# The device loop over the middle tiles of a fused Mamba and mixture-of-experts layer, written out as one straight list of steps on every engine

## The reference

```python
x = x + mamba(layernorm(x));  x = x + moe(layernorm(x))

def mamba(x):
    u, res = split(x @ W_in);  u = silu(u)
    delta = softplus(u @ W_delta + b_delta);  Bm = u @ W_B;  Cm = u @ W_C
    h = exp(delta * A) * h + delta * Bm * u          # a scan over the 256 tokens, for 16 states
    y = sum over states of h * Cm, plus u * D_param
    return (y * silu(res)) @ W_out

def moe(x):
    gate = x @ Wg.T + routing_bias
    weights = softmax over the 4 largest of 8 gates
    return swiglu(x, Ws1, Ws2, Ws3) + sum_e weights[e] * swiglu(x, W1[e], W2[e], W3[e])
    # swiglu(u, w1, w2, w3) = (silu(u @ w1.T) * (u @ w2.T)) @ w3.T
```

## Time and profile before

| what | value |
|---|---|
| three runs | 1539.65, 1535.20, 1539.01 us; median 1539.01 us |
| the profiled execution, whole | 1535.95 us |
| its span, first to last instruction | 1534.1 us |
| what lies around the span | 1.85 us |
| granted TensorE clock, mean | 0.988 of full speed |
| PE busy | 1473.8 us, 96% of the span |
| DVE busy | 1413.0 us, 92% |
| ACT busy | 1230.3 us, 80% |
| POOL busy | 850.2 us, 55% |

### The profile page before, as it was taken

How to read it: one execution, slowest core, us unless ns; L and a number is a source line. 1 busy time by engine, 2 the same in 40 slices (tenths; PEclk the granted TensorE clock), 3 DMA queues, 4 the chain that set the end, 5 groups by cost and what they waited for, 6 DMA issues and landing times. The chain is left out here.

```text
span 1534.1 us, 31186 instructions
## 1 busy us (share of the span) xinstructions
PE 1473.8 (96%) x9510; PEld 1245.7 (81%) x9510; DVE 1413.0 (92%) x2834; ACT 1230.3 (80%) x1841; POOL 850.2 (55%) x508
## 2 busy tenths in 40 slices
PE   4879999999999999999999999999999999999998
PEld 3677887888788887888879788887978888898887
DVE  5869999999999999999999999999999999999843
ACT  5978888888789798888979888897988889787331
POOL 5965564665456376555647556564755657375100
PEclk7999999999999999999999999999999999999999
DMA  5320212112111211211121131112202120201000
GB/s 183 95 99 22 74 34 81 43 57 77 35 57 43 90 41 37 95 35 56 42 90 41 36 96 35 56 42 70 87 10 87 46 63 29 98 15 57 1 8 8
DMA packets 50482, 87.02 MB, mean 57 GB/s; under 512 B 4663, under 2 KB 32820, under 8 KB 50356
## 3 DMA queue, kind: packets, MB, share of 16 engines
q1 hardware_dynamic: 49556, 82.52, 16.6%
q10 hardware_dynamic: 800, 3.14, 0.6%
HBM read 80.93 MB, written 4.72 MB: 56 GB/s over the span
## 5 line engine op out<-in xcount | busy, mean ns | idle before, releaser
L641 POOL TENSOR_TENSOR hb<-soft,bbc 128x1024 f32<-128x1024 f32 x256 | 628.2, 2479 | 21.4 <-DMA bbc<-b_rows 18.3
L1131 PEld LDWEIGHTS eo_bank<-w_sb,gated 128*128 128x128 f32 x3840 | 470.5, 192 | 30.6 <-issue 17.5
L1131 PE MATMUL eo_bank<-w_sb,gated 128*128 128x128 f32 x3840 | 488.2, 276 | 2.7 <-DVE o L937 1.9
L861 DVE SCALAR_TENSOR_TENSOR acc<-turn,c_sb,acc 128x256 f32<-128x256 f32 x900 | 375.9, 474 | 13.3 <-issue 10.6
L696 ACT ACT_TABLE_LOAD x299 | 383.6, 1283 | 5.4
L849 DVE TENSOR_TENSOR_SCAN hb<-decay_bank,hb 128x512 f32<-128x512 f32 x256 | 310.7, 1214 | 24.3 <-POOL hb L641 14.1
L1064 PE MATMUL turn<-ident,hb 128*128 128x128 f32 x2048 | 291.6, 275 | 36.1 <-DVE hb L849 16.9
L794 ACT ACTIVATE s<-h 128x512 f32<-128x512 f32 x384 | 221.8, 598 | 126.8 <-PE h L1115 121.0
L849 DVE TENSOR_TENSOR_SCAN hb<-decay,hb 128x512 f32<-128x512 f32 x256 | 318.3, 1274 | 2.0 <-ACT decay L776 1.8
L1064 PEld LDWEIGHTS turn<-ident,hb 128*128 128x128 f32 x2048 | 241.9, 142 | 82.8 <-issue 22.5
L928 DVE TENSOR_TENSOR gated<-h,s 128x512 f32<-128x512 f32 x384 | 253.5, 678 | 28.0 <-PE h L1115 17.6
(11 more groups left out here) (105 smaller groups left out, 1511.2 us busy)
## 6 DMA issues: line engine op xcount, KB each, us to landing
bbc<-b_rows SPq DMA_DIRECT2D x128, 512.0 KB, 5.1
x_in<-x_dram SPq DMA_DIRECT2D x16, 256.0 KB, 3.0
x_cur<-x_dram SPq DMA_DIRECT2D x16, 256.0 KB, 6.3
out_dram<-o SPq DMA_DIRECT2D x15, 256.0 KB, 2.5
gated<-w_all_dram ACTq DMA_DIRECT2D x1, 1534.5 KB, 8.6
hb<-w_all_dram ACTq DMA_DIRECT2D x1, 1534.5 KB, 12.4
w_sb<-w_all_dram SPq DMA_DIRECT2D x5, 192.0 KB
b_rows<-cbT SPq DMA_DIRECT2D x16, 32.0 KB, 1.6
```

Of the source, the lines that this page charges most:

```text
L641: pool.tensor_tensor(hb[:, arg % HB_RING, :, :], du[:, h, :].unsqueeze(1).broadcast_to((P, GN, TOK)), bbc[:, r, :].rearrange("p (n t) -> p ...
L861: dve.scalar_tensor_tensor(acc[:, blk, :], turn_bank[pair][:, i * DI:(i + 1) * DI], c_sb[:, blk, n:n + 1], acc[:, blk, :], ALU.mult, ALU.add)\
L1131: mm = pe.matmul(eo_bank[:, blk * P:(blk + 1) * P], gated[:, k % GATED_RING, blk * P:(blk + 1) * P], w3_sb[:, pair, :], start=(n == 0), st ...
```

## The change

`bodies` now builds one Python list for each engine: the head, then the body nine times with the numbers of its tiles filled in for j = 6 to 14, then the tail. `program` is called once with that list. The tables are the same, so each engine executes the same steps in the same order. What falls away is the device loop itself, all register instructions that computed wait values and addresses in the body, and the special cases at the seams of head, body and tail (which activation table ACT holds there, and which step last used the shared PSUM bank `side` on PE).

```diff
         def bodies(eng, engine, program):
 
             head, body, tail = ORDER[engine]
-            program([((tile, 0), step, arg) for tile, step, arg in head], None)
-            with eng.Fori(*LOOP) as j:
-                program([((j, SHIFT[part]), step, arg) for part, step, arg in body], body)
-            program([((tile, 0), step, arg) for tile, step, arg in tail], body)
+            program([((tile, 0), step, arg) for tile, step, arg in head]
+                    + [((j + SHIFT[part], 0), step, arg) for j in range(*LOOP) for part, step, arg in body]
+                    + [((tile, 0), step, arg) for tile, step, arg in tail])
...
-            def program(entries, before):
-                table = table_after(before, None) if before else EXP_TABLE
-                head = before is None
+            def program(entries):
+                table = EXP_TABLE
                 for turn, step, arg in entries:
...
-                wanted = table_after(ORDER["act"][1], None)
-                if head and table != wanted:
-                    act.preload_act_table_set(wanted)
-
...
-            def program(entries, before):
-                if before is None:
-                    last = None
-                elif isinstance(entries[0][0][0], int):
-                    last = last_side(before, lambda part: (LOOP[1] - 1, SHIFT[part]))
-                else:
-                    side_free(last_side(ORDER["pe"][0], lambda tile: (tile, 0)))
-                    last = last_side(before, lambda part: (entries[0][0][0], SHIFT[part] - 1))
+            def program(entries):
+                last = None
                 for turn, step, arg in entries:
```

More of the change, by code:

```diff
@@ L975, in side_free @@
                     wait_before(pe, reader, turn, per, GATE_STEPS if step == "gate" else arg + 1)
-            def last_side(entries, turn_of):
-                uses = [(turn_of(at), step, arg) for at, step, arg in entries if step in SIDE]
-                return uses[-1]
             def stay_busy(times):
```

## The result

The changed kernel takes 1522.61 us (median of six runs, 1519.87 to 1526.93). Six runs of the kernel before, the three shown above and three beside the changed one, have a median of 1537.57 us (1535.20 to 1540.35). The ratio is 0.9905, with a 95% interval of 0.9887 to 0.9924: about 1% faster. The prediction had the direction right and the size too small.

The account below looks back on a forecast made before the run. PE and DVE, both nearly full in the eight looped passes, were taken as the bound. Only DVE's jumps counted: 8 x 1.29 = 10.3 us off 1539.01 gives 1528.7 us, range about 1524 to 1534 us.

Parts of the forecast that it names:

- The jump back on DVE, eight times, removed: At DVE's loop jump in the middle: removing the code fetch saves 1.29 us a pass, 10.3 us in all.
- The register steps ... Counted at nothing: In the loop body, 140 a pass on DVE and 83 on PE: hidden behind queued work, so removal gains nothing.
- What is late next. PE ... the gain cannot go beyond the 1.29 us: In each middle pass: without the stall PE's own 88.66 us bounds, so the gain stops at 1.29 us.
- Rival 4: In the passes: fewer sequencer steps let DVE and PE start earlier; 88.4 us a pass, gain 12.4 us; chance 0.08.
- Head and tail ... stays: Outside the loop: time unchanged, including PE's 3.03 us wait for ACT's sres before the first pass.
- Straight code must be fetched ... at nothing: In the written-out passes: PE fetches about 5 blocks each, 40 more in all, at no cost.
- Rival 3: In the written-out passes: PE's code blocks arrive late, about 1.3 us each; with two a pass 1549.5 us; chance 0.04.
- The jumps of PE, ACT, POOL and SP: At the other engines' loop jumps: removing them counted at nothing.
- Rival 2: At DVE's stall on sum: it comes with the place, not the jump, and stays; 1538 us; chance 0.05.

Follow-up runs that it names:

- e1: The kernel before, loops kept, without PE's one wait between head and loop body; 1532.13 us, ratio 0.9971.
- e4: The kernel before without PE's wait at the loop's entry, with a prefetch hint on DVE's loop jump; 1528.26 us, ratio 0.9941.
- e8: The changed kernel, but PE loops with a body of three passes and so jumps back twice; 1527.46 us, ratio 0.9919.
- e5: The changed kernel with PE's wait for ACT's sres put back where the head ends; 1527.75 us, ratio 0.9923.
- e2: The kernel before with only DVE's list written out straight; other engines' loops and PE's entry wait stay; 1526.18 us, ratio 0.9919.
- e9: The kernel before without PE's entry wait, DVE's loop cut right behind three queued scans, seven jumps; 1534.26 us, ratio 0.9980.
- e12: The kernel of e9 with DVE's loop head placed at the start of a code block; 1523.30 us, ratio 0.9917.
- e7: The changed kernel, but DVE loops with a body of three passes and so jumps back twice; 1524.58 us, ratio 0.9900.

## Why the prediction was right or wrong

**"The jump back on DVE, eight times, removed": right, and priced somewhat high.** Measured alone (from e1 to e4) it is 1.15 us a pass, between PE's visible wait of 1.10 us and the 1.29 us taken. The 1.29 us was the difference between a later pass and the first; with the wait of PE gone too (e1) it is 89.891 - 88.63 = 1.26 us. The Trainium skill, page "Advanced Engine Details and Errata", section Control Flow Timing, has some 108 ns for a compare-and-branch, which by itself would be 0.9 us in all. The runs disagree with that as the price of a jump whose target is not at hand: 1.15 us each here, 3.9 us each on PE in e8.

**"The register steps ... Counted at nothing": wrong, and the step that made the passes too long.** They cost 0.23 to 0.27 us a pass on DVE, about 2 us in all. The 1.467 us that a pass lost are 1.15 for the fetch, 0.23 for DVE's register steps, 0.03 for the other engines (no more than noise), and 0.05 by which the profiles of before and e1 differ. The "proof" was a mistake of method. I took the first pass as the changed kernel in small and PE's lack of idle time in it as a sign that the steps were covered. But the first pass has the register steps too, so comparing it with a later one cannot show them. And "never idle" is not "as fast as it can be": its 88.66 us became 88.36 without a listed wait of PE having been there to remove. What went were the delays of under 0.1 us by which DVE let PE go late.

**"What is late next. PE ... the gain cannot go beyond the 1.29 us": wrong for the same reason.** PE's 88.66 us were not PE's own. Its matmuls alone need at most the 88.48 us of the changed kernel. Rival 4, which let DVE and PE start earlier for want of sequencer steps and had 88.43 us a pass, had the mechanism and the pass (to 0.05 us), and with its 12.4 us it was closer than the forecast; it had been given 0.08.

**"Head and tail ... stays": wrong, and the step that put the result outside the range.** I read `ACT sres` in the bracket of the earlier trace rows as a dependence of the data. It was a wait emitted at the seam, and the diff shows its removal in PE's program. What the profile names as the releaser says whose event ended the wait, not that the wait is needed. e1 and e5 measure it: 3.2 and 3.0 us in the profiles. With these 3.2 us still there the median would be about 1525.8 us, inside the range.

**"Straight code must be fetched ... at nothing": right.** 38 blocks on q8 in the eight passes, and PE has no listed wait. Rival 3 (late blocks, slower) did not occur. The Trainium skill, page "Runtime: NRT & Kernel Launch", section Instruction fetch mechanics, says that fetching the next block of straight code is mostly hidden, and the changed profile agrees: 38 packets and no wait of PE.

**"The jumps of PE, ACT, POOL and SP": right**, at most 0.03 us a pass with their register steps (e2). For PE that holds only while its body is kept; e8 shows the other side.

**Rival 2, the stall comes with the place:** false. Straight code has none at the same step, and when the jump was moved (e9) the stall moved with it.

Put together: 10.3 forecast, plus 1.4 (passes), plus 3.2 (seam), plus 0.3 (first pass) is 15.2 us; the start's +1.2 us and the rest's -0.3 make it 14.4 in the spans. Those are 4.1 us more than forecast. Between the forecast of 1528.7 us and the median of 1522.61 us lie 6.1 us: 1.4 us more come from the three added runs of the kernel before, which lowered its median, and 0.6 us from the difference between a profiled execution and a median.

## What to carry to other kernels

To price a jump, look at when the engine's sequencer does its next step, and set against it how much work is queued on the engine there; only the difference is lost. Where a loop has to stay, putting the jump right behind long instructions, and the loop's head at the start of a block of code, is worth a try: in this kernel e12 got a looped body to within 0.27 us a pass of straight code. On two engines that are both nearly full, an empty list of waits does not show that neither delays the other; the starts of the same instruction in two traces do. And read every removed line of a diff that emits a wait, also at seams: a wait that the profile puts down to another engine's work may be an instruction that nothing needs.

## What the runs showed that I had not expected

- A wait of some 3 us of TensorE is sometimes followed by several microseconds at half the clock, and sometimes not. After 3.04 us of idle time e2 fell to 0.59 and 0.50 and lost 2.5 us more, and after 2.43 us e8 fell to 0.59 and lost 1.4 us; the kernel before, after 3.03 us, and e5, after 2.8 us, stayed at 1.00. What decides it stays open.
- The stop behind a jump was 3.4 to 3.6 us on DVE in the kernel before, 2.8 to 2.9 us in e7, 3.1 to 3.4 us in e9, 2.8 to 2.9 us and once 3.4 us in e12, and 3.3 to 3.8 us on PE in e8 (3344 and 3752 ns).
- The prefetch hint took nearly all fetches of DVE's code out of the loop, not only that of the jump (49 packets on q14 in eight passes became one), and a stop of 4.1 us came 35 us behind the loop.
- A second stop of 2 us can follow the first when the jump's target lies badly in its block (e9, gone in e12). This pair shows that the placing is the cause; which instruction crossed a block's edge was not looked up.
